# A two-layer transformer block on one core: weights' loads moved to ScalarE's queue, values copied a fill later, two stores exchanged, four down pieces placed elsewhere

## The reference

```python
# layer 0
h = x * rsqrt(mean(x*x) + 1e-6) * (w1 * (1 + cond @ tw1.T))
q, k, v = h @ Wq.T, h @ Wk.T, h @ Wv.T      # 8 query heads of 64, 1 key/value head
x = x + softmax(rope(q) @ rope(k).T / 8) @ v @ Wo.T
h = x * rsqrt(mean(x*x) + 1e-6) * (w2 * (1 + cond @ tw2.T))
x = x + (silu(h @ Wg.T) * (h @ Wu.T)) @ Wd.T # 2048 inner features: the dense part
# layer 1
h = layernorm(x) * (1 + scale(cond)) + shift(cond)
q, c = h @ Wq.T, h @ Wkd.T                   # 16 query heads of 32
k, v = c @ Wku.T, c @ Wvu.T                  # 4 key/value heads
out = x + softmax(rope(q) @ rope(k).T / sqrt(32)) @ v @ Wo.T
```

## Time and profile before

| what | value |
|---|---|
| time, median of 3 runs | 880.28 us (877.74 to 880.79) |
| profiled execution, time | 880.93 us |
| profiled execution, span from first to last instruction | 879.1 us |
| TensorE busy | 849.0 us |
| VectorE busy | 603.2 us |
| ScalarE busy | 443.9 us |
| GpSimd busy | 404.8 us |
| SP's transfers | 112.45 MB, 40.3% of the 16 DMA engines' span |

### The profile page before, as it was taken

The page is one execution under the profiler, slowest core; times in us unless marked ns, Lnnn a source line. Parts: engine busy times, 40 slices in busy tenths (PEclk is TensorE's granted clock), DMA queues, the critical chain, the costliest instruction groups (busy, mean ns, idle before and its releaser), DMA issues.

```text
span 879.1 us, 15477 instructions
## 1 busy us (share of the span) xinstructions
PE 849.0 (97%) x5864; PEld 706.8 (80%) x5864; DVE 603.2 (69%) x877; ACT 443.9 (50%) x819; POOL 404.8 (46%) x320
## 2 busy tenths in 40 slices
PE   8898999999999999999999899999999999999997
PEld 5686888888888888888787788888878878878885
DVE  6686466766765666666457787876766857767874
ACT  3665444454444454444457546455454464445652
POOL 1456546445454545547357545445343444422331
PEclk9899999999999999999999999999999999999998
DMA  9811534534523534524534445536346255230001
GB/s 350 331 36 39 178 105 135 160 102 136 162 99 111 162 108 114 162 96 120 192 119 128 135 136 167 171 106 188 113 143 181 83 171 151 71 104 13 26 26 37
DMA packets 114297, 113.53 MB, mean 129 GB/s; under 512 B 57520, under 2 KB 80048, under 8 KB 114224
## 3 DMA queue, kind: packets, MB, share of 16 engines
q1 hardware_dynamic: 113504, 112.45, 40.3%
q10 hardware_dynamic: 720, 0.09, 0.1%
HBM read 88.15 MB, written 24.38 MB: 128 GB/s over the span
## 4 chain that ended last, share of the span: by engine, by line
PE 67%; DVE 9%; issue 7%; DMA 6%; ACT 6%; POOL 4%; SPq 1%; POOLq 0%; ACTq 0%; DVEq 0%
PE ps L685 20%; PE ps L687 20%; PE ps L686 20%; DMA turned_q<-tq 3%; DMA qkT<-turned_q 2%; PE ps L799 2%; DVE ex L1411 2%; POOL gul L545 1%; PE ps L965 1%; PE ps L731 1%; PE ps L942 1%; DVE t L1239 1%; DVE ex L1283 1%; ACT ah L1767 1%; ACT L1761 1%
## 5 line engine op out<-in xcount | busy, mean ns | idle before, releaser
L685 PE MATMUL ps<-h2h,guh 128*128 128x512 f32 x512 | 204.7, 400 | 4.4 <-issue 2.2
L687 PE MATMUL ps<-h2l,guh 128*128 128x512 f32 x512 | 199.8, 390 | 0.0
L686 PE MATMUL ps<-h2h,gul 128*128 128x512 f32 x512 | 199.6, 390 | 0.0
L545 POOL TENSOR_TENSOR gul<-rgu,guh 128x1024 fp32r<-128x1024 f32 x64 | 160.4, 2507 | 65.7 <-ACT guh L1748 65.7
L550 POOL TENSOR_TENSOR wdl<-rwd,wdh 128x512 fp32r<-128x512 f32 x64 | 82.8, 1293 | 159.1 <-ACT wdh L1756 158.9
L1310 DVE TENSOR_TENSOR xres<-ps,xres 128x512 f32<-128x512 f32 x128 | 87.5, 684 | 64.5 <-PE ps L687 64.0
L685 PEld LDWEIGHTS ps<-h2h,guh 128*128 128x128 f32 x512 | 96.1, 188 | 27.2 <-issue 6.9
L687 PEld LDWEIGHTS ps<-h2l,guh 128*128 128x128 f32 x512 | 96.1, 188 | 21.0
L686 PEld LDWEIGHTS ps<-h2h,gul 128*128 128x128 f32 x512 | 96.2, 188 | 19.1
L1300 DVE TENSOR_TENSOR af<-ps,sg 128x512 f32<-128x512 f32 x64 | 44.2, 690 | 88.2 <-PE ps L687 46.8
L685 PE MATMUL ps<-wdh,ah 128*128 128x512 f32 x256 | 100.8, 394 | 1.8 <-DVE al L1305 1.8
(11 more groups left out here) (178 smaller groups left out, 1701.7 us busy)
## 6 DMA issues: line engine op xcount, KB each, us to landing
rgu<-gu SPq DMA_DIRECT2D x64, 512.0 KB, 3.9
rwd<-WdT SPq DMA_DIRECT2D x64, 256.0 KB, 4.0
turned_q<-tq SPq DMA_DIRECT2D x20, 320.0 KB, 2.2
qkT<-turned_q SPq DMA_DIRECT2D x20, 320.0 KB, 3.6
turned_p<-tp SPq DMA_DIRECT2D x9, 512.0 KB, 2.6
pT<-turned_p SPq DMA_DIRECT2D x9, 512.0 KB, 3.9
xt<-xT SPq DMA_DIRECT2D x16, 256.0 KB, 3.5
out<-xres SPq DMA_DIRECT2D x15, 256.0 KB, 3.5
```

The lines of the kernel that those rows point to most:

```text
L545: pool.tensor_tensor(gul[i][:, :], rgu[i][:, :], guh[i][:, :], ALU.subtract).then_inc(m_gul, 1)
L685: pe.matmul(dst, lh, rh, start=start, stop=False)
L686: pe.matmul(dst, ll, rh, start=False, stop=False)
L687: return pe.matmul(dst, lh, rl, start=False, stop=stop)
```

## The change

Four edits. First, all loads of the pieces from SP's generator `mlp()` are issued by ScalarE: SP's generator and its fills are gone, `load_gate_up` and `load_down` stand in ScalarE's queue inside its own generator, with the same semaphores. Loads 0 to 3 of gate and up and 0 and 1 of down stay on SP. Second, `values(s + 1)` stands behind the first fill in steps s > 4 of layer 0, and `values1(u + 1)` behind the second fill in steps u < 9 of layer 1. Third, in layer 0 VectorE transposes the second norm's tile (`turn_x2`) after the probabilities, and SP stores and fetches the probabilities ahead of it. Fourth, the last four down pieces: before, two stood in the first fill of step 9, ahead of QKV of tile 10, and one on each side of the probabilities' transpose; now two stand behind QKV of tile 10 and two behind the transpose (on VectorE, their adds stand behind the rope product).

```diff
-FILL1 = {-1: (4, 4, 0, 4, 0), **{u: (4, 2, 2, 2, 2) for u in range(0, 9)}, 9: (2, 0, 0, 0, 0)}
+FILL1 = {-1: (4, 4, 0, 4, 0), **{u: (4, 2, 2, 2, 2) for u in range(0, 9)}, 9: (0, 0, 0, 0, 0)}
@@ sync: mlp() and every fill(pieces, ...) removed
+                probs_away(s)
                 if moved:
                     x2_away(ready)
-                probs_away(s)
+                probs_back(s)
                 if moved:
                     x2_back(ready)
-                probs_back(s)
@@ tensor
                 if u == TAIL:
-                    fill(pieces, 1)
+                    fill(pieces, 2)
                     p_T1(u)
-                    fill(pieces, 1)
+                    fill(pieces, 2)
@@ vector
                 softmax_sub(s)
                 moved = ready is not None and ready >= TURN_X2
-                if moved:
-                    turn_x2(ready)
@@
                 if s >= TURN_P0:
                     turn_probs(s)
+                if moved:
+                    turn_x2(ready)
                 if in_layer(s + 1):
                     rope_mul(s + 1)
@@
-                if u == TAIL:
-                    fill(pieces, 1)
                 if in_layer(u + 1):
                     rope_mul1(u + 1)
                 if u == TAIL:
+                    fill(pieces, 2)
                     probs_T1(u)
-                    fill(pieces, 1)
+                    fill(pieces, 2)
                     stats1(u + 3)
@@ scalar
+            def load_gate_up(n):
+                if n < NN:
+                    act.wait_ge(m_gul, n - 1)
+                    act.dma_start(rgu[n % 2][:, :], gu[n % NG, :, :]).then_inc(ld_gu[n % 2], 16)
+
+            def load_down(n):
+                if n < NN:
+                    g = n % NG
+                    act.wait_ge(m_wdl, n - 1)
+                    act.dma_start(rwd[n % 2][:, :], WdT[g * P:(g + 1) * P, :]).then_inc(ld_wd[n % 2], 16)
@@ scalar, mlp()
                     yield
                     if p:
                         yield
+                        load_gate_up(2 * p + 3)
+                        load_down(2 * p + 1)
                     yield
                     high_act(2 * p)
@@
                     silu(2 * p + 1)
+                    load_down(2 * p + 2)
                     yield
                     if p:
                         yield
+                    load_gate_up(2 * p + 4)
                     yield
                     high_wd(2 * p + 1)
@@ scalar, layer 0
-                if in_layer(s + 1):
+                if s <= HEAD and in_layer(s + 1):
                     values(s + 1)
                 if s == NT - 1:
                     norm1(0)
                 fill(pieces, f1)
+                if s > HEAD and in_layer(s + 1):
+                    values(s + 1)
@@ scalar, layer 1
-                if in_layer(u + 1):
+                if u >= TAIL and in_layer(u + 1):
                     values1(u + 1)
                 fill(pieces, f2)
+                if u < TAIL:
+                    values1(u + 1)
```

More of the change, by code:

```diff
@@ L291, in load_down @@
                     sp.dma_start(rwd[n % 2][:, :], WdT[g * P:(g + 1) * P, :]).then_inc(ld_wd[n % 2], 16)
[L293 to L313, removed]
             def away(tile, to, cols, signal):
@@ L428, in _ @@
             for s in range(HEAD, NT):
-                f1, f2, f3 = FILL0.get(s, (0, 0, 0))
                 ready = PREP0.get(s)
@@ L438, in _ @@
                 moved = ready is not None and ready >= TURN_X2
+                probs_away(s)
                 if moved:
                     x2_away(ready)
-                probs_away(s)
+                probs_back(s)
                 if moved:
                     x2_back(ready)
-                probs_back(s)
-                fill(pieces, f1)
                 if in_layer(s + 1):
@@ L450, in _ @@
                     y_away(0)
-                fill(pieces, f2)
                 if s == NT - 1:
@@ L455, in _ @@
                     sp.dma_start(w1st[:, :].rearrange("p (k n) -> p k n", k=KT), by_row(Wo1T)).then_inc(ld_w1, 16)
-                fill(pieces, f3)
                 if s == NT - 2:
@@ L461, in _ @@
             for u in range(-1, NT):
-                f1, f2, f3, f4, f5 = FILL1.get(u, (0,) * 5)
                 ready = PREP1.get(u)
@@ L465, in _ @@
                     x2_away(ready)
-                fill(pieces, min(f1, 2))
                 if ready is not None:
                     x2_back(ready)
-                fill(pieces, f1 - min(f1, 2))
                 if 0 <= u < TAIL:
@@ L483, in _ @@
                     store(u - 1)
-                fill(pieces, f3 + f4 + f5)
             for h in range(2):
```

## The result

| | before | after |
|---|---|---|
| time, median | 880.53 us (877.74 to 881.98, 4 runs) | 889.12 us (887.6 to 891.49, 4 runs) |
| profiled execution, time | 880.93 us | 888.45 us |
| its span | 879.1 us | 886.7 us |
| mean granted TensorE clock of its span | 0.99 | 0.99 |

The ratio is 1.0105, with a 95% interval of 1.007 to 1.014: the change makes the kernel slower by 1%, outside the range of the forecast. It falls in the case that had a chance of 0.13, and at the place that this rival named.

A forecast was written before the change was run, and what follows sets the result against it. TensorE, busy 849.0 of 879.1 us, was taken as the bound, so only its idle counted. From 880.93, -1.3 - 2.7 + 3.2 - 1.6 = -2.4 gave 878.5, or 877.9 us against the median; range 871.5 to 884.5.

The forecast's parts named there:

- the forecast's price of the probabilities' way back: Layer 1, even tiles 0 to 6: loads moving beside the probabilities' return make TensorE wait, +3.2 us, bounds 0 and 6.8.
- The price d of a meeting: Layer 1: delay of the probabilities' return when 512 KB and then 256 KB move beside it, 0.9 us, between 0 and 1.8.
- The second rival: Layer 1: queues take turns, loads cost full engine time, 1.9 us per even tile, 8.7 in all; 883.4 us, chance 0.12.
- The cover: Layer 1: spare time before the probabilities' use, 0.4 us in tile 2; odd tiles' 0.6 us meeting counted as covered.
- the queries' term: Layer 1: queries return sooner, ending waits ahead of tiles 1, 3 and 5, -2.7 us; tile 0's 1.36 us wait stays.
- The first pair: First groups on ScalarE: each load's wait for GpSimd's low part two groups back is already over, cost 0.
- Values later: Layer 0, steps 6, 8, 12 and 14: TensorE's four silu waits of 0.32 us go, -1.3 us.
- Stores' order: Layer 0: probabilities transposed and stored ahead of the second norm's tile, cost 0.
- Issues on ScalarE: ScalarE's queue: 122 load issues of 0.46 us add 56 us of its time, costed at 0.
- The tail: Last four down pieces: a wait and half clock go, new gaps come, -1.6 us, bounds 0 and -3.5.
- the fourth rival's case: Last down pieces: the clock falls in the new gaps, so the tail gives nothing; 879.5 us, chance 0.09.
- The third rival: Layer 1, TensorE's context: late probabilities make the kernel slower by over 0.5%, needing d = 2.2; chance 0.13.

The follow-up runs named there:

- the last experiment: The changed kernel with loads back on SP at their old places and the tail's first down add ahead of the rope product: 870.73 us, ratio 0.9897.
- the last four kernels: Changed kernel variants: SP loads ahead of the probabilities' fetch, 897.4 us; both ways back free, 872.78 (SP) and 873.01 (ScalarE); SP loads, first down add earlier, 870.73.
- the two kernels with both ways back free: Changed kernel, loads kept off the queries' and probabilities' ways back, tile 0's queries and first down add earlier: 872.78 us (loads on SP), 873.01 us (on ScalarE).

## Why the prediction was wrong

The step that failed is the forecast's price of the probabilities' way back, +3.2 us in place of 8.9, in three ways.

- **The moment.** A load was to go "as soon as silu, weight copy and values are through": 0.4 us ahead of the way back in tile 0, and 0.3 to 1.3 us behind it in tiles 2, 4 and 6. It went 1.6, 0.9, 1.4 and 0.9 us ahead. In tile 2 the load stands in ScalarE's queue behind the silu, the weight copy and the values' copy, and yet:

```profile
564.78 0.60 ACT L1740 ACTIVATE sg<-ps 128x512 f32<-128x512 f32 x1 [6.96 <-PE ps L656]
565.02 0.33 ACTq L1729 DMA_DIRECT2D rgu<-gu  x1
565.28 0.61 ACT L1724 CAST wdh<-rwd 128x512 fp32r<-128x512 f32 x1
...
565.79 1.08 ACT L1839 COPY bdv<-ps 64x128 f32<-64x128 f32 x4
```

The values are through at 566.87, 1.0 us behind the way back's issue at 565.89, just where the forecast had the load. The load was issued 1.85 us before that, as soon as the waits ahead of it were over and while the work ahead of it still ran. In tiles 4 and 6 it is 1.8 us too, in tile 0 1.1. So its bytes moved beside the way back from its start on, and not from a quarter of it on. What the same load would have cost at the forecast's moment was not measured.

- **The price d of a meeting**, taken as 0.9 for 512 and 256 KB together, "with half of it falling into free slots". In even tiles the landing is 1.3 to 2.2 us later, 1.7 on average, and the wait grows by 1.3 to 1.7. 512 KB alone cost 0.9. The free slots were there (29% of the engines' time), but the loads' packets took 2.75 us of it, not the 1.9 of a full-rate stream. The second rival had the price nearly right, 1.9 us. That its sum of 8.7 us meets the 8.9 is in part luck: the even tiles grew by 7.75, and the rest is tile 3, which it had at 0.
- **The cover.** Tile 3 was priced 0 (odd tiles, 256 KB) and lost 1.2 us: there the 256 KB load is issued 0.2 us ahead of the way back and the 512 KB load, which was to miss most of it, 0.4 us behind; it lands in 6.4 instead of 4.5. Tile 8 was counted with the even tiles only in the rivals. It meets 256 KB alone and lands 2.2 us later. In tiles 1, 5 and 7 both loads come 0.2 and 0.7 us behind, the landing is 0.8 to 1.3 us later, and the cover held: no wait.

Two smaller terms were costed at nothing and weren't:

- **Tile 0's queries**, "it stays", for no load was ahead of them. One comes behind them now, and beside them on another queue that counts as well: +2.7 us. That eats the whole gain of the queries' term, which was itself right: the waits ahead of tiles 1, 3 and 5 are gone (-2.7), and the queries' store lands in 3.4 to 4.1 us in tiles 0, 2, 4 and 6.
- **The first pair**, where "by the order of the pieces" GpSimd was to be done. It is in the steady order, not where the dense part begins: 2 us of ScalarE and, with the values' copy moved behind them, 1.1 of TensorE.

The other terms:

- **Values later**: -1.3 forecast, and the four silu waits went.
- **Stores' order**: 0, and nothing shows against it; it was not run alone.
- **Issues on ScalarE**: 0, and outside the first pair TensorE waits for ScalarE nowhere longer than before. The issues took 47 us, not 56.
- **The tail**: -1.6 forecast. Where the clock held it gave -1.7 and -1.8. In the changed kernel the two gaps (0.61 and 1.13 us) were followed by a stretch at half clock, the fourth rival's case, and it gave 0.15:

```profile
804.80:808.20 3.40, 3.40 (x10) 2.63 (x9) 1.28 (x2) 0.51 (x1) 0.56 (x1) 0.50 0.00 0
```

From the forecast for the profiled execution, 880.93 - 2.4 = 878.5, to its 888.45: context +5.7, clock behind the long waits of layer 1 +4.1, queries +2.7, tail +1.5, first pair +1.1, the two ends -4.2, and -1.0 in layer 0 that its terms don't explain. That is 9.9 of 9.95. The third rival named place and sign, and wanted d = 2.2 for it to be slower. In fact d was 1.7 on average, and the rest came of the terms that it took from the forecast as gains: of 5.6 us, the queries gave 0 in sum and the tail 0.15.

## What to carry to other kernels

Before a transfer is moved to another queue, ask which transfer on a short chain (store, fetch, use) is in flight at its new moment: here one or two loads, up to 768 KB, beside a 512 KB way back made its landing 1.5 us later on average over nine tiles, where at most 0.4 us was spare in the even ones, though the DMA engines were busy only 40% of the span. Loads with pieces to spare belong behind such a fetch, and behind the next chain's fetch too; which engine issues them mattered by nothing that could be measured (872.8 and 873.0 us). Don't count on the work ahead of an issue to hold it back: here only the waits ahead of it did. When a moved issue waits for another engine, check the first round, where the steady order doesn't hold yet.

## What the runs showed of the hardware

**ScalarE issues a transfer while the work ahead of it in its queue still runs.** In tiles 2, 4 and 6 a load is issued 0.24 us after the silu ahead of it has started, and before the weight copy and the values' copy ahead of it have. 45.5 of the 47 us of issues lie beside work of ScalarE. So ScalarE's queue keeps its order for waits and for work, but an issue doesn't wait for the work ahead of it to end. Where a wait stands ahead of an issue, the work behind it is held up too: 2 us at 93.6.

**VectorE and GpSimd slow each other, and whoever starts first is faster.** The multiply of tile 0's probabilities by VectorE takes 3.4 us in the changed kernel, and 1.2 where it starts 0.15 us ahead of GpSimd's subtraction; then this one takes 3.3 instead of 2.6. The changed kernel, GpSimd and VectorE:

```profile
486.76 2.63 POOL L514 TENSOR_TENSOR gul<-rgu,guh 128x1024 fp32r<-128x1024 f32 x1 [0.18 <-ACT guh L1716]
...
487.05 3.42 DVE L1380 TENSOR_TENSOR ex<-ex,smx 128x1024 f32<-128x1024 f32 x1
```

and the last experiment:

```profile
484.29 1.21 DVE L1411 TENSOR_TENSOR ex<-ex,smx 128x1024 f32<-128x1024 f32 x1
...
484.44 3.33 POOL L545 TENSOR_TENSOR gul<-rgu,guh 128x1024 fp32r<-128x1024 f32 x1 [0.62 <-ACT guh L1749]
```

In the first pair VectorE ends 1.1 us after GpSimd does (489.39), about its own 1.2, as if it had started only then; in the second GpSimd takes 0.7 us longer and ends 2.3 us after VectorE (485.50).

The Trainium skill, "Trainium Architecture — The Big Picture", section What this means for kernel authors, calls the port that the two share an exclusive lock and no split of bandwidth; the trace agrees, with 3.42 us against 1.21.

The multiply takes 3.3 to 3.4 us in the tiles 1 to 8 of every kernel here (but for one of 2.95), and 1.2 in the tail and in tile 0 of the last four kernels. It stands on the chain that ends at the context, so up to 2.2 us a tile might be had there where the context waits. That was not tried, and a fast multiply alone doesn't end the wait: in the two kernels with both ways back free, tile 0's takes 1.22 us and its context still waits 3.2.

**The clock spreads the runs.** The kernel before took 876.0 us at a mean granted clock of 0.996 and 882.9 at 0.988: 0.008 x 880 = 7 us, which is of the size of the best gains above. Stretches of 3.4 us at half clock stand at the three longest waits of the changed kernel (at 473.7, 501.0 and 712.6 us). But a wait's length alone doesn't tell: in the kernel with the tail's edit alone waits of 1.8 us have such a stretch behind them (475.4 and 649.5), while the 2.52 us wait before and the waits of 3.2 and 3.3 us in the two kernels with both ways back free have none.

**One landing is longer in nearly every kernel.** The probabilities' way back of tile 6 takes 5.2 us before, where most tiles take 3.8 (tile 3 4.5), and 5.2 as well where the loads stand behind the context; in the two kernels with both ways back kept free it is 3.8 to 3.9. No run tells why.
